# Attention's folded output weights by fp16 products of values and remainders, in a Trainium2 kernel of channel attention and patch matching

## The reference

```
x = x + attention(groupnorm(x))          # the stage that the change touches
x = x + motif(groupnorm(x))              # patch matching, untouched

def attention(x):
    qkv = conv1x1(x, w_qkv) + b_qkv      # 96 -> 288
    qkv = depthwise3x3(qkv, w_dw) + b_dw
    q, k, v = split(qkv)                 # 4 heads of 24 channels
    q, k = q / |q|, k / |k|              # over all 16384 pixels
    attn = softmax((q @ k.T) * temperature)      # 24 x 24 per head
    return conv1x1(attn @ v, w_out) + b_out
```

## Time and profile before

| | |
|---|---|
| median of three executions | 1478.48 us (1476.63 to 1479.1) |
| span of the profiled execution | 1473.2 us, first to last instruction |
| that execution's own whole time | not recorded apart; the median is 5.3 us over the span |
| PE, share of the span | 89% |
| DVE, ACT, POOL | 77%, 60%, 45% |
| mean granted clock of TensorE | 0.956 of full |
| first half of attention | about 52 to 253 us (image 0), 779 to 975 us (image 1) |
| fold and first output unit | from 262 us (image 0), from 983 us (image 1) |

### The profile page before, as it was taken

One profiled execution on the slowest core, in us unless ns is written; L12 is line 12 of the kernel. 1 busy time (PEld: TensorE's weight loads), 2 busy tenths in 40 slices (PEclk: granted clock), 3 DMA queues, 4 the chain that ended last, 5 costly groups with the idle time before them and its releaser, 6 DMA issues. The chain is left out here.

```text
span 1473.2 us, 34011 instructions
## 1 busy us (share of the span) xinstructions
PE 1317.6 (89%) x13586; PEld 1057.6 (72%) x13586; DVE 1140.7 (77%) x1896; ACT 887.0 (60%) x1013; POOL 656.8 (45%) x672
## 2 busy tenths in 40 slices
PE   3899998996899499999989999999959968999998
PEld 1789997996899355555548899879949954555554
DVE  6577777368873599999976777755887839999998
ACT  3566664211553299999965556532135508999996
POOL 4888894243220144534019888814412113444400
PEclk9999999898999699999999999999979978999999
DMA  5466631494215343553438866309405225274533
GB/s 212 125 190 195 204 108 52 121 315 139 88 52 208 140 146 92 160 132 111 119 104 245 250 207 187 84 19 281 123 1 216 109 91 184 78 188 108 147 72 103
DMA packets 75876, 210.27 MB, mean 143 GB/s; under 512 B 15306, under 2 KB 15414, under 8 KB 72646
## 3 DMA queue, kind: packets, MB, share of 16 engines
q1 hardware_dynamic: 61214, 158.10, 34.0%
q0 software_dynamic: 6720, 36.93, 9.3%
q10 hardware_dynamic: 7784, 13.07, 3.3%
HBM read 91.54 MB, written 67.04 MB: 108 GB/s over the span
## 5 line engine op out<-in xcount | busy, mean ns | idle before, releaser
L1771 PE MATMUL acc<-rnd,ident 128*128 128x376 f32 x1152 | 391.8, 484 | 15.9 <-ACT rnd L1748 15.9
L1771 PEld LDWEIGHTS acc<-rnd,ident 128*128 128x128 f32 x1152 | 217.0, 192 | 136.3 <-ACT rnd L1748 17.3
L956 PE MATMUL ps_a<-wa,xa 128*128 128x192 f16 x1536 | 296.2, 247 | 9.0 <-DMA xc<-low 6.9
L956 PE MATMUL ps_a<-wb,xb 128*128 128x192 f16 x1536 | 295.0, 246 | 0.0
L1743 ACT ACTIVATE rnd_m<-prod,plus_round,scale 128x1504 f32<-128x1504 f32 x144 | 235.8, 1637 | 43.1 <-DVE prod L1592 32.5
L574 POOL TENSOR_TENSOR vt<-z 96x256 f32<-96x256 f32 x248 | 254.7, 1047 | 4.2 <-ACT z L850 4.0
L1707 DVE SCALAR_TENSOR_TENSOR over<-prod,scale,rnd 128x1504 bf16<-128x1504 f32 x144 | 256.5, 1784 | 0.0
L1748 ACT ACTIVATE rnd<-rnd_m,minus_round 128x1504 f32<-128x1504 f32 x144 | 223.2, 1550 | 4.7
L1651 POOL DMA_INDIRECT near<-f_planes,index x42 | 122.8, 2923 | 146.2 <-DVE prod L1592 139.7
L956 PEld LDWEIGHTS ps_a<-wa,xa 128*128 128x128 f16 x1536 | 150.4, 98 | 12.3 <-DMA xc<-low 8.3
L956 PE MATMUL ps_a<-wfa,xa 128*128 128x96 f16 x1536 | 157.7, 207 | 1.7 <-issue 1.6
(11 more groups left out here) (338 smaller groups left out, 2468.8 us busy)
## 6 DMA issues: line engine op xcount, KB each, us to landing
xb<-xa ACTq DMA_DIRECT2D x64, 195.0 KB, 2.7
f_planes<-img SPq DMA_DIRECT2D x8, 1536.0 KB, 13.9
fc<-f_planes SPq DMA_DIRECT2D x16, 768.0 KB, 5.7
v_a<-xa SPq DMA_DIRECT2D x40, 260.0 KB, 2.6
v_b<-xb SPq DMA_DIRECT2D x40, 260.0 KB, 3.1
xa<-v_a SPq DMA_DIRECT2D x40, 260.0 KB, 4.4
xb<-v_b SPq DMA_DIRECT2D x40, 260.0 KB, 5.1
v_c<-xc SPq DMA_DIRECT2D x40, 195.0 KB, 3.4
```

The lines of the kernel that those rows point to most:

```text
L956: mm = lambda a, w, first, end: nc.tensor.matmul(out(i), a, w, start=first, stop=end)
L1771: nc.tensor.matmul(o(m), k["ident"][:, :], rnd[:, n % RNDS, BR * m:BR * m + BR, :], start=False, stop=False, skip_group_check=True)
```

## The change

The laid-out weights, `mix` and the output bias become pairs of fp16 arrays, a value (index 0) and what is left after it (index 1), in the same room as the fp32 arrays before. `mix` and the bias are scaled by 64 first, and the copies of the folded weights scale back. A product of the fold is now three fp16 products: value x value, value x remainder, remainder x value. PE folds the two inner lines, convolves the inner lines of unit 0, folds the outer lines, and convolves the outer ones; before, all four folds came first. DVE makes the weights' remainders in units 10 to 21 of the first image (`lay_low`, after `qk_low(2u+1)`), the remainder of `mix` after ACT's copy of it, and for `wfc` two dependent operations in place of one. POOL makes the remainders of the bias columns in `prepare`.

```diff
@@ prepare, POOL
             for first in (C, C + 3):
-                nc.gpsimd.tensor_copy(k["wv_c"][:, :, first:first + 3], v_bias[:].rearrange("p (i v) -> p i v", v=3))
+                last = nc.gpsimd.tensor_copy(k["wv_c"][:, 0, :, first:first + 3], v_const)
+            last.then_inc(zeroed, 1)
+            pool.wait_ge(zeroed, DIAG + 4)
+            for first in (C, C + 3):
+                nc.gpsimd.tensor_tensor(k["wv_c"][:, 1, :, first:first + 3], v_const,
+                                        k["wv_c"][:, 0, :, first:first + 3], ALU.subtract)
@@ attention
-        mix = sb("mix", [C, C], F32)
+        mix = sb("mix", [C, 2, C], F16)
@@ attention, DVE
+            def lay_low(t):
+                i, d = divmod(t, 3)
+                by = k["taps_v"][:, t:t + 1]
+                dve.wait_ge(laid, t + 1)
+                if t == 0:
+                    nc.vector.scalar_tensor_tensor(k["b_split"][:, 1, :], k["b_out"][:, :], MSCALE,
+                                                   k["b_split"][:, 0, :], ALU.mult, ALU.subtract)
+                hi, lo = k["wv_u"][:, 0, t], k["wv_u"][:, 1, t]
+                for to, of, less in ((lo[:, 0:C], slice(0, C), hi[:, 0:C]), (lo[:, C:WV], slice(0, WV - C), hi[:, C:WV]),
+                                     (k["wv_c"][:, 1, i, 32 * d:32 * d + 32], slice(64, C),
+                                      k["wv_c"][:, 0, i, 32 * d:32 * d + 32])):
+                    nc.vector.scalar_tensor_tensor(to, k["w_v"][:, of], by, less, ALU.mult, ALU.subtract)
@@
                 qk_low(2 * u + 1)
+                if b == 0 and 10 <= u < 22:
+                    lay_low(u - 10)
@@
+            dve.wait_ge(att_act, 3)
+            nc.vector.scalar_tensor_tensor(mix[:, 1, :], ps[0][0:C, 1, 0:C], MSCALE, mix[:, 0, :], ALU.mult,
+                                           ALU.subtract).then_inc(mix_lo, 1)
             for r, i in enumerate(LINES):
@@
-                nc.vector.tensor_tensor(wfb[0:C, taps, :], taps_of(wide[i])[0:C], wfa[0:C, taps, :], ALU.subtract
-                                        ).then_inc(wf_split, 1)
+                nc.vector.scalar_tensor_tensor(wfb[0:C, taps, :], taps_of(wide[i])[0:C], 1.0 / MSCALE,
+                                               wfa[0:C, taps, :], ALU.mult, ALU.subtract).then_inc(wf_split, 1)
                 dve.wait_ge(att_act, 3 + 3 * r + 3)
-                nc.vector.scalar_tensor_tensor(wfc[C:XCR, i, :], wfc[C:XCR, i, :], k["minus_low"][C:XCR, 0:1],
-                                               tail_of(rest[i])[C:XCR], ALU.mult, ALU.add).then_inc(wf_split, 1)
+                c.then_wait(nc.vector.tensor_scalar(wfc[C:XCR, i, :], wfc[C:XCR, i, :], k["minus_low"][C:XCR, 0:1],
+                                                    None, ALU.mult))
+                nc.vector.scalar_tensor_tensor(wfc[C:XCR, i, :], tail_of(rest[i])[C:XCR], 1.0 / MSCALE,
+                                               wfc[C:XCR, i, :], ALU.mult, ALU.add).then_inc(wf_split, 1)
@@ attention, ACT: lay_out
+                if t == 0:
+                    nc.scalar.activation(k["b_split"][:, 0, :], k["b_out"][:, :], ACT.Copy, scale=MSCALE)
...
+                last.then_inc(laid, 1)
@@ attention, PE
             pe.wait_ge(att_act, 3)
-            for i in LINES:
+            pe.wait_ge(mix_lo, 1)
+
+            def fold(i):
+                terms = ((0, 0), (0, 1), (1, 0))
                 for dx in range(3):
                     for bank, first in ((wide[i], 0), (rest[i], 32)):
-                        nc.tensor.matmul(bank[:, C * dx:C * dx + C], k["wv_u"][:, 3 * i + dx, first:first + P], mix[:, :],
-                                         start=True, stop=True)
+                        for w_, m_ in terms:
+                            nc.tensor.matmul(bank[:, C * dx:C * dx + C], k["wv_u"][:, w_, 3 * i + dx, first:first + P],
+                                             mix[:, m_, :], start=(w_ == 0 and m_ == 0), stop=(w_ == 1))
                 centre = i in (1, 2)
                 if centre:
-                    nc.tensor.matmul(tail_of(rest[i])[0:XCR], k["last_row"][:, i - 1, :], k["b_out"][:, :], start=True,
-                                     stop=False)
-                nc.tensor.matmul(tail_of(rest[i])[0:XCR], k["wv_c"][:, i, :], mix[:, :], start=not centre, stop=True
-                                 ).then_inc(att_pe, 1)
+                    for m_ in range(2):
+                        nc.tensor.matmul(tail_of(rest[i])[0:XCR], k["last_row"][:, i - 1, :], k["b_split"][:, m_, :],
+                                         start=(m_ == 0), stop=False)
+                for w_, m_ in terms:
+                    last = nc.tensor.matmul(tail_of(rest[i])[0:XCR], k["wv_c"][:, w_, i, :], mix[:, m_, :],
+                                            start=(not centre and w_ == 0 and m_ == 0), stop=(w_ == 1))
+                last.then_inc(att_pe, 1)
@@
             for lines in (INNER, OUTER):
+                for i in LINES[0:2] if lines == INNER else LINES[2:4]:
+                    fold(i)
                 for j in range(2):
                     last = conv(at(0, j), ORDER[0], slot_out[0], j, lines, wfa, wfb, wfc,
                                 ready=weights_in if j == 0 else None)
```

More of the change, by code:

```diff
@@ L60 @@
 WV = C + 64
+MSCALE = 64.0
 V_TERMS = ((0, 2, ALU.subtract), (1, 2, ALU.add), (2, 1, ALU.subtract), (3, 1, ALU.subtract))
@@ L285, in _ @@
             pool.wait_ge(zeroed, DIAG + 3)
+            v_const = v_bias[:].rearrange("p (i v) -> p i v", v=3)
             for first in (C, C + 3):
-                nc.gpsimd.tensor_copy(k["wv_c"][:, :, first:first + 3], v_bias[:].rearrange("p (i v) -> p i v", v=3))
+                last = nc.gpsimd.tensor_copy(k["wv_c"][:, 0, :, first:first + 3], v_const)
[4 more added lines that the diff above has]
+                                        k["wv_c"][:, 0, :, first:first + 3], ALU.subtract)
             nc.gpsimd.memset(k["edge"][0:C, :], 0.0)
@@ L409 @@
             "outs", "o_s", "o_t", "o_a", "evac") \
-    + ("rows_ready0", "rows_ready1", "parts_in0", "parts_in1", "parts_in2", "saved0", "saved1", "saved2",
+    + ("laid", "mix_lo") + ("rows_ready0", "rows_ready1", "parts_in0", "parts_in1", "parts_in2", "saved0", "saved1", "saved2",
        "dup_in0", "dup_in1", "dup_in2")
@@ L462, in attention @@
          att_pe, att_act, wf_split, pivot_in, pivot_out, outs, o_s, o_t, o_a, evac) = (sems[n] for n in ATT_SEMS[:34])
+        laid, mix_lo = sems["laid"], sems["mix_lo"]
         rows_ready = [sems[f"rows_ready{j}"] for j in range(2)]
@@ L880, in lay_out @@
                 by = k["taps_v"][:, t:t + 1]
-                for to, of in ((k["wv_u"][:, t, 0:C], slice(0, C)), (k["wv_u"][:, t, C:WV], slice(0, WV - C)),
-                               (k["wv_c"][:, i, 32 * d:32 * d + 32], slice(64, C))):
-                    nc.scalar.activation(to, k["w_v"][:, of], ACT.Identity, scale=by)
+                if t == 0:
+                    nc.scalar.activation(k["b_split"][:, 0, :], k["b_out"][:, :], ACT.Copy, scale=MSCALE)
+                for to, of in ((k["wv_u"][:, 0, t, 0:C], slice(0, C)), (k["wv_u"][:, 0, t, C:WV], slice(0, WV - C)),
+                               (k["wv_c"][:, 0, i, 32 * d:32 * d + 32], slice(64, C))):
+                    last = nc.scalar.activation(to, k["w_v"][:, of], ACT.Identity, scale=by)
+                last.then_inc(laid, 1)
             act.wait_ge(turned, 1)
@@ L919, in _ @@
             act.wait_ge(att_pe, 3)
-            nc.scalar.activation(mix[:, :], ps[0][0:C, 1, 0:C], ACT.Copy).then_inc(att_act, 1)
+            nc.scalar.activation(mix[:, 0, :], ps[0][0:C, 1, 0:C], ACT.Copy, scale=MSCALE).then_inc(att_act, 1)
             for r, i in enumerate(LINES):
@@ L923, in _ @@
                 act.wait_ge(att_pe, 4 + r)
-                nc.scalar.activation(wfa[:, taps, :], taps_of(wide[i]), ACT.Copy).then_inc(att_act, 1)
-                nc.scalar.activation(wfb[C:P, taps, :], taps_of(rest[i])[C:P], ACT.Copy).then_inc(att_act, 1)
-                nc.scalar.activation(wfc[:, i, :], tail_of(rest[i])[0:XCR], ACT.Copy).then_inc(att_act, 1)
+                nc.scalar.activation(wfa[:, taps, :], taps_of(wide[i]), ACT.Copy, scale=1.0 / MSCALE).then_inc(att_act, 1)
+                nc.scalar.activation(wfb[C:P, taps, :], taps_of(rest[i])[C:P], ACT.Copy, scale=1.0 / MSCALE
+                                     ).then_inc(att_act, 1)
+                nc.scalar.activation(wfc[:, i, :], tail_of(rest[i])[0:XCR], ACT.Copy, scale=1.0 / MSCALE
+                                     ).then_inc(att_act, 1)
             for n in range(UNITS):
@@ L1802, in build @@
             stats=sb("stats", [P, GN, NQ + 1, 6], F32), dev=sb("dev", [P, GN, 2 * NQ], F32),
-            wv_u=sb("wv_u", [C, 12, WV], F32), wv_c=sb("wv_c", [C, 4, XCR], F32),
-            last_row=sb("last_row", [1, 2, XCR], F32), minus_low=sb("minus_low", [P, 1], F32),
+            wv_u=sb("wv_u", [C, 2, 12, WV], F16), wv_c=sb("wv_c", [C, 2, 4, XCR], F16),
```

(1 more changed line is left out.)

## The result

| | before | changed | changed over before |
|---|---|---|---|
| first comparison, medians of 6 | 1478.79 us (1476.63 to 1480.02) | 1487.6 us (1482.27 to 1493.97) | 1.0056 [1.0032, 1.0079] |
| second comparison, another chip | 1475.29 us | 1490.88 us (1486.12 to 1497.45) | 1.0126 [1.007, 1.0182] |
| span of the profiled execution, first comparison | 1473.2 us | 1482.5 us (whole time 1484.28) | |
| PE, DVE, share of the span | 89%, 77% | 89%, 78% | |

The change makes the kernel slower. The predicted 1489.3 us lies 1.7 above the first median. That closeness is luck: the two large terms of the sum were wrong by some 6 and 9 us, in opposite directions. Shares over the whole span show nothing of it; the stages do.

What follows compares the result with a forecast made beforehand. First-half pace was set by the ring of DVE, ACT and POOL, the fold by PE. 16.3 (lay_low) - 0.7 (hidden wait) + 0.6 - 5.4 (folds) = 10.8 us on 1478.5 gave 1489.3 us, range 1476 to 1494.

Steps and rivals of the forecast that it cites:

- the two large terms of the sum: lay_low in the first image's first half, 16.3 us slower, and the first image's fold, 5.4 us faster.
- the ring of DVE, ACT and POOL: First half of attention: these engines hand each other a unit every 6.11 us and hold PE (5.75) back.
- I take 1.36, the unit with the two `own_block` operations: lay_low in 12 units of the first image: 1.36 us a unit, taken from an earlier unit, 16.3 us in all.
- One turn: Rival for lay_low: POOL gets in once per unit, 1.0 x 12 = 12.0 us, total 1485.0 us; chance 0.24.
- the prediction's upper case: lay_low: POOL gets in twice between the operations, 0.4 + 2 x 0.6 = 1.6 us a unit.
- One block: Rival for lay_low: its three operations run together, 0.4 x 12 = 5.0 us, total 1478.0 us; chance 0.14.
- The wait for saved rows: First half: ACT's waits before reusing a slot (4.9 us together) partly shrink, hiding 0.7 us (0 to 2.3).
- The fold at full clock: From the old PE start to the first outer_rows: 10.7 us against 10.10, so 0.6 slower in the second image.
- the new order puts two chains of copies on the path where the old one hid three of four: Fold: why it would be 0.6 us slower at full clock although PE does its fold in half the time.
- The gain of 5.4 in the first image: First image's fold: 10.7 us against 16.17, 5.4 faster if the granted clock stays full, otherwise 2.7.
- No gain in the fold: Rival: the clock drops in both images because PE idles in four places; 1494 us; chance 0.06 with another rival.
- Preparation: Before the first units: added POOL subtractions and ACT's lay-out cost 0, at most 0.5 us; `b_split` 0 to 0.3.

Runs made afterwards that it cites:

- no_low: Changed kernel without lay_low, the remainders of value weights and bias set to zero: 1477.8 us, 1.0031 of before.
- one_input: Changed kernel with lay_low's three operations replaced by three one-input tensor_reduce of the same sizes, remainders zero: 1476.99 us (one execution).
- late: Changed kernel with lay_low moved to units 28 to 31 and behind the last pair of the first image: 1478.95 us, 1.003 of before.
- filled: Changed kernel with products of zeros in PE's four pauses of the fold: 1485.53 us, 1.0073 of before.
- folds_first: Changed kernel with all four folds ahead of unit 0's convolution, as before the change: 1480.95 us, 1.0019 of before.
- late_first: Changed kernel with the edits of late and folds_first together: 1469.46 us, 0.9973 of before.
- after: Changed kernel with no further edit, its profile from the first comparison: span 1482.5 us, whole time 1484.28 us.
- changed_again: Changed kernel with no further edit, run again on another chip for a second profile: 1490.88 us, 1.0126 of before.

## Why the prediction came out as it did

**lay_low: right in kind, mis-sized.** The prediction said that the ring of DVE, ACT and POOL sets the pace, that three small operations move it by more than their own length, and that the reason is POOL. All of it holds (`no_low`, `one_input`). The failed step is "I take 1.36, the unit with the two `own_block` operations": it measured 0.99 in units 11 to 21. The mechanism was that of the rival *One turn* (1.0 a unit). That its price came out to 0.01 is luck: it took the work for 0.4, which is 0.74 (`late`), and didn't take off the 0.40 that `td` had waited before. The other two counts of turns happened too: two in unit 16 of `filled`, at 1.57 (the prediction's upper case was 1.6), and none in unit 10, at 0.75 with a fourth operation, so that *One block* at 0.4 was too cheap. The better scale stood in the same row as the worse: `td` waits 0.40 in every unit, and that wait is given to the new operations, so a wait is added only where POOL gets in once more. From the rows: alone the operations take 0.50 and 0.24 (`late`), here 0.84 and 0.71, so they wait 0.34 for POOL's `td` and 0.47 for its `vt`. That is 0.81 of waiting in place of 0.40, and 0.74 of work; the sum is 1.15, and what it has over the measured 0.99 is the overlap of operations in the record. The row taken for the scale was itself a unit with two turns. POOL's timeline beside the `own_block` of the earlier trace rows, in the kernel before:

```profile
92.40 1.40 POOL L574 TENSOR_TENSOR vt<-z 96x256 f32<-96x256 f32 x2
```

Both `vt` end at 93.80, and DVE's `td` ends 0.21 later, at 94.01. That each `own_block` reads its scalar from memory may be why POOL got in twice; no run tried it.

**The wait for saved rows: more was hidden than taken.** I took 0.7 off. Of the stall of the one unit, 7.46 - 6.11 = 1.35, nothing shows in the slower ring, where that unit takes 7.13 as its neighbours do; unit 9, ahead of the twelve, was 0.4 shorter. Twelve units add 10.1, the first half 9.8, against 15.6 in the sum (16.3 - 0.7).

**The fold at full clock: right within 0.4 us at every step, 0.2 at the end.** Counted from the old PE start (271.03 = end of `mix`'s copy and 0.05), PE starts at 0.37 (forecast 0.36), convolves line 1 at 3.66 (3.38), line 2 at 4.92 (4.56), has line 3's weights at 9.67 (9.6), and `outer_rows` comes at 10.92 (10.7). What was short is the time to ACT's first copy of line 1, 1.83 for 1.56. PE folds a line without a bias row in 0.91 us (276.85 to 277.76) where it took 1.52 (987.42 to 988.94 before): six tenths, not the half that the prediction says. The sentence "the new order puts two chains of copies on the path where the old one hid three of four" is what `folds_first` shows: 2.8 us an image at full clock.

**The gain of 5.4 in the first image: the failed step.** "First image: 10.7 against 16.17 is 5.4 faster" took the half clock of one profile for a property of the old fold. In the first pair of profiles the difference did come out (-5.25), but by luck: the kernel before shows the half clock in 1 of 6 folds. What the profiles show of the two kernels is the opposite. The rival *No gain in the fold* was given too little: with PE's four pauses (3.0 us in all in the first image) the clock fell in 9 of 14 folds, and filling them kept it in 4 of 4. The mean fold is 12.87 - 11.40 = 1.5 us longer, and 2.3 with the 0.8 behind the first `outer_rows`, not 2.4 shorter.

**Preparation: 0 was said, and it came out shorter.** ACT's lay-out and POOL's two subtractions show nowhere. The first `y_s` comes at 54.89 to 55.00 in the three profiles of the kernel before and at 53.55 to 54.23 in the nine of kernels with the whole change, 1.0 sooner in the mean. Why isn't shown.

**The sum, corrected.** 9.8 + 2 x 2.3 - 1.0 = 13.4 us. The medians say +8.8 and +15.6; by the intervals of the ratios it is 4.7 to 11.7 in the first comparison, which the 13.4 misses, and 10.3 to 26.9 in the second. The weakest part is the 11.40: without its one fold at half clock the sum would be 15.4. The predicted +10.8 was 15.6 + 0.6 - 5.4: too much by 5.8 in the first half and by 1.0 in the preparation, too little by 9.4 in the folds (+4.6 for -4.8). Reckoned in the same way, `filled` should be 9.8 - 0.1 - 1.0 = 8.7 over before and is 0.0073 x 1474 = 10.8 [6.6, 14.7]. `late_first` should gain 2 x (11.40 - 9.02) + 1.0 less 0.7 in its unit 28, 5.1 in all, and measured 0.0027 x 1475 = 4.0 [0.9, 7.1], 5.8 by the medians.

Of the second halves, the +0.6 of the second image is the 0.9 between its first two `outer_rows`, less 0.3 behind them. Left open: the +0.8 of the first and about 1.3 us elsewhere, which single profiles don't settle (the kernel before alone takes 80.7 to 85.1 us for that second half in its three profiles); and why a fold with pauses sometimes keeps the clock. The Trainium skill (TensorE: Matmul & The Clock Gate, "A second HAM failure mode: psum-queue depth-cycling") tells of a kernel in which short idle moments between groups of matmuls made the clock go back and forth; the 0.98, 0.54, 0.95, 0.55 above look like it, and no run here tells what decides between the two outcomes.

## What to carry to other kernels

Before small operations are put into a ring that two engines share, ask of each whether it has two inputs in memory that the other engine reads too, and what the other has queued: with one input three of them cost nothing here, with two even one cost a turn where the other engine had work queued, and in the last units, where the other engine had nothing queued, they cost 0.7 us in one unit and nothing in the others. When work on an engine becomes faster, look at what its old length hid: here copies, which is why folding all lines first beats folding each pair when it is needed. And don't book a gain from a clock seen in one profile; take that stretch from several executions, and where an engine's pauses put its clock at risk, try filling them: it kept the clock here, though the whole time hasn't shown the gain yet.

## What the runs showed of the hardware that was not expected

- Three one-input operations, 0.46 us long together, cost 0.00 us a unit; `td` waits 0.40 there anyway.
- The turns between DVE and POOL are nearly regular: 7.09 to 7.14 us in units 11 to 21 of `after`, `changed_again`, `folds_first` and `filled`, but for one unit in 44, where POOL got two turns. In unit 10, with a fourth small operation in front, POOL got none.
- An operation on DVE that ends 0.11 us after POOL's `td` (139.32 against 139.21) isn't followed by DVE's next two-input operation: POOL's next one goes first, and DVE's `td` takes 0.88 for 0.34.
- With products of zeros in pauses of 0.6 to 1.0 us the granted clock stayed 1.00 in four folds of four, for 0.1 us a fold; without them it fell in 9 of 14 before the fold's end.
